# Token attention's front: weight shares split one block earlier, batch 0 values from kept transposes in two shares, two score maxima for a value tile

## What is computed

```python
def _attn_block(q_src, k_src, v_src, Wq, Wk, Wv, Wo, bo):
    q = _split_heads(q_src @ Wq)
    k = _split_heads(k_src @ Wk)
    v = _split_heads(v_src @ Wv)
    dots = jnp.einsum('bhid,bhjd->bhij', q, k) * SCALE
    attn = jax.nn.softmax(dots, axis=-1)
    out = jnp.einsum('bhij,bhjd->bhid', attn, v)
    ...
    return out @ Wo + bo
out = x1 + _attn_block(x1, x2, x2, Wq, Wk, Wv, Wo, bo)   # x2: 77 context rows
return _attn_block(out, out, x1, Wq, Wk, Wv, Wo, bo)     # 1024 tokens
```

## Time and profile before

| | |
|---|---|
| Time, median of 3 runs | 2435.78 us (2428.44 to 2436.41) |
| Time of the profiled execution | 2444.54 us |
| Its span in the trace | 2442.7 us |
| Granted TensorE clock, mean over the span | 0.964 |
| PE busy | 2296.2 us, 94% |
| DVE busy | 1509.2 us, 62% |
| ACT busy | 1107.7 us, 45% |
| POOL busy | 1062.4 us, 43% |

### The profile page before, as it was taken

How to read it: one execution, slowest core, us unless ns; L and a number is a source line. 1 busy time by engine, 2 the same in 40 slices (tenths; PEclk the granted TensorE clock), 3 DMA queues, 4 the chain that set the end, 5 groups by cost and what they waited for, 6 DMA issues and landing times.

```text
span 2442.7 us, 34142 instructions
## 1 busy us (share of the span) xinstructions
PE 2296.2 (94%) x12934; PEld 1439.0 (59%) x12934; DVE 1509.2 (62%) x2289; ACT 1107.7 (45%) x2370; POOL 1062.4 (43%) x780
## 2 busy tenths in 40 slices
PE   8999999889988999999999999999899789979998
PEld 4333443267754555555655554787566657768887
DVE  6788688267745666665666666713344566565556
ACT  2577677733323444442344444433322477643323
POOL 2556547423443888883578786333301122100000
PEclk6999999899999999999999999999899899989999
DMA  6534432232110011111011111354301511020001
GB/s 132 142 85 97 80 62 64 71 82 39 1 18 1 11 15 14 15 32 40 1 15 15 11 15 19 79 160 104 87 1 37 142 31 38 1 65 14 1 1 35
DMA packets 137805, 114.21 MB, mean 47 GB/s; under 512 B 74565, under 2 KB 114995, under 8 KB 137257
## 3 DMA queue, kind: packets, MB, share of 16 engines
q1 hardware_dynamic: 100585, 111.61, 16.8%
q0 software_dynamic: 36864, 0.15, 4.4%
q10 hardware_dynamic: 192, 0.26, 0.0%
HBM read 85.99 MB, written 13.39 MB: 41 GB/s over the span
## 4 chain that ended last, share of the span: by engine, by line
PE 76%; DMA 9%; DVE 8%; ACT 4%; issue 2%; SPq 1%; POOL 1%; ACTq 0%; POOLq 0%; DVEq 0%
PE PS L128 73%; DMA adj<-e_EE,e_IX 8%; PE PS L1287 1%; ACT a_P L884 1%; DVE c_MX L1935 1%; DVE g_SS L132 1%; PE PS L360 1%; SPq L154 1%; DVE c_AC L132 0%; DVE g_st L1378 0%; DVE a_MX L759 0%; ACT g_SS L1472 0%; PE PS L361 0%; DMA a_s<-a_OU 0%; POOL e_EQ L137 0%
## 5 line engine op out<-in xcount | busy, mean ns | idle before, releaser
L353 POOL DMA_INDIRECT adj<-e_EE,e_IX x256 | 416.1, 1625 | 416.0 <-DMA adj<-e_EE,e_IX 355.7
L1935 DVE TENSOR_REDUCE c_MX<-PS 128x2 f32<-128x1024 f32 x256 | 312.9, 1222 | 176.6 <-PE PS L128 176.4
L132 POOL TENSOR_TENSOR c_AC<-c_AC,c_P 128x1024 f32<-128x1024 f32 x145 | 364.8, 2516 | 70.7 <-DVE c_AC L132 63.9
L2032 ACT ACTIVATE c_P<-PS 128x1024 f32<-128x1024 f32 x256 | 252.0, 1026 | 215.1 <-PE PS L128 215.1
L759 DVE TENSOR_REDUCE a_MX<-PS 128x2 f32<-128x1024 f32 x256 | 304.0, 1219 | 55.6 <-PE PS L128 54.2
L884 ACT ACTIVATE a_P<-PS 128x512 f32<-128x512 f32 x512 | 270.1, 602 | 91.0 <-PE PS L128 90.0
L128 PE MATMUL PS<-c_P,c_VV 128*64 128x512 f32 x1024 | 247.7, 605 | 0.0
L137 POOL TENSOR_SCALAR e_EQ<-e_KR,e_KC 128x128 bf16<-128x128 f32 x256 | 165.0, 645 | 144.9 <-DMA e_KR<-adj_key 92.9
L128 PE MATMUL PS<-a_QS,a_KS 64*128 64x512 f32 x512 | 194.3, 464 | 11.2 <-ACT a_P L884 6.7
L128 PEld LDWEIGHTS PS<-a_QS,a_KS 64*128 64x128 f32 x512 | 84.3, 190 | 165.7 <-ACT a_P L884 97.5
L128 PE MATMUL PS<-a_KS,a_QS 48*128 48x512 f32 (+1 forms) x512 | 168.6, 473 | 11.2 <-DVE a_MX L759 11.1
(11 more groups left out here) (499 smaller groups left out, 4595.9 us busy)
## 6 DMA issues: line engine op xcount, KB each, us to landing
e_KR<-adj_key SPq DMA_DIRECT2D x64, 256.0 KB, 3.7
f_W<-in_L_ffn_w SPq DMA_DIRECT2D x16, 1024.0 KB, 7.8
c_RB<-c_r SPq DMA_DIRECT2D x58, 128.0 KB, 2.9
g_FB<-in_fside_1x16xSxS SPq DMA_DIRECT2D x8, 616.0 KB, 8.0
adj<-e_zt SPq DMA_DIRECT2D x16, 256.0 KB, 4.1
adj<-e_EE,e_IX POOLq DMA_INDIRECT x256, 3.2
d_AJ<-adj SPq DMA_DIRECT2D x8, 512.0 KB, 9.0
a_KS<-a_KH SPq DMA_DIRECT2D x30, 128.0 KB, 3.7
```

The source lines that it names most:

```text
L132: return v.e.tensor_tensor(o, a, b, op)
L353: g.e.indirect_dma_start(self.adj, bass.IndirectOffsetOnAxis(ap=self.IXE[:, k:k + 1], axis=0), self.EE[:, k:k + 1], None, compute_op=ALU.a ...
L1935: v.e.reduce_max(MX[:, w % 2, :, qt, kh], bank(0, 2).rearrange("p (h n) -> p h n", h=2), AX, negate=True).then_inc(*smax_dve.up())
L2032: s.e.activation(PB[t % NP][:, :, :].rearrange("p h n -> p (h n)"), bank(2 + 2 * (t % 2), 2), ACT.Exp, scale=0.125).then_inc(*st_act.up())
```

## The change

It makes a class `Shares` before block b, used in both blocks, and changes five things.

1. `coarse` and `fine` of the weights of P = 0 are done in block b, at i = 13 and 14 (`shares`).
2. x1's transposes of batch 0 (XT, columns 0 to 1023) are split into two shares c_XV in block b, at i = 2 to 5, 512 columns of one half of the depth at a time (`x_shares`), before c_XH takes their place. c_XV lies in a part of c_OT.
3. In the front, WV is split into shares c_WV, over the buffers c_P, in two halves of 512 columns (`split_v`), between the first preparations of keys and queries.
4. Values of batch 0 are products in shares: 6 fp32r matmuls for a tile and half. `turn_x` for batch 0 is gone. The second half is a job of its own, `prep_w`.
5. Round 0's maxima are made two for a tile, in tiles 0 to 3; `row 0` and `m 0` follow in tile 4, and round 1's first four maxima in tiles 4 to 7. The P = 1 weights are split in tiles 4 and 5.

```diff
@@ stage_ctx, schedule
+                if 2 <= i < 6:
+                    yield "x_shares", (i - 2) // 2, i % 2
+                if 13 <= i < 15:
+                    yield "shares", 14 - i
...
+class Shares:
+    def __init__(self, K):
+        W = K.over("c_WS", "LS", 0, [128, 2, 2, 2, 128])
...
+        self.XV = [K.over(f"c_XV{n}", "c_OT", 8192 * i + 8192, [128, 2, 1024]) for i, n in enumerate("HL")]
...
+    def coarse(self, s, P, w):
+        for k in range(2):
+            ins = s.e.copy(self.WS[w][0][:, k, :], self.weight(w, P, k))
+        ins.then_inc(*self.act.up())
...
+    def coarse_x(self, s, k, h):
+        cols = slice(512 * h, 512 * h + 512)
+        s.e.copy(self.XV[0][:, k, cols], self.XT[:, k, cols]).then_inc(*self.x_act.up())
+    def fine_x(self, v, k, h):
+        cols = slice(512 * h, 512 * h + 512)
+        v.wait_ge(self.x_act, 2 * k + h + 1)
+        tt(v, self.XV[1][:, k, cols], self.XT[:, k, cols], self.XV[0][:, k, cols].bitcast(F32), ALU.subtract).then_inc(*self.x_dve.up())
@@ stage_c, schedule
-        for w in (1, 0):
-            yield "coarse", 0, w
-            yield "fine", 0, w
         yield "prep_k", 0, 0
+        yield "split_v", 0
         yield "prep_q", 0
+        yield "split_v", 1
         yield "prep_k", 0, 1
         yield "prep_q", 1
         for b in range(2):
-            if b == 0:
-                yield "turn_x", b, 0
             for kt in range(8):
                 if b and kt == 0:
                     continue
-                if kt < 7:
+                if b and kt < 7:
                     yield "turn_x", b, kt + 1
                 yield "prep_v", b, kt
                 if kt < 6:
                     yield "send", 2
-                if b == 0:
-                    yield "s", 0, kt
-                    if kt >= 4:
-                        yield "s", 1, kt - 4
-            for w in (1, 0):
-                yield "coarse", 8 * b + 1, w
-                yield "fine", 8 * b + 1, w
+                if b == 0 and kt < 4:
+                    yield "s", 0, 2 * kt
+                yield "prep_w", b, kt
+                if b == 0 and kt < 4:
+                    yield "s", 0, 2 * kt + 1
+                elif b == 0:
+                    if kt == 4:
+                        yield "row", 0
+                        yield "m", 0
+                    yield "s", 1, kt - 4
+                    if kt < 6:
+                        yield "coarse", 1, 5 - kt
+                        yield "fine", 1, 5 - kt
             if b:
+                for w in (1, 0):
+                    yield "coarse", 8 * b + 1, w
+                    yield "fine", 8 * b + 1, w
                 yield "fetch", 2
-            if b == 0:
-                yield "row", 0
-                yield "m", 0
-            else:
...
@@ stage_c, tensor
+                    pe.wait_ge(K.shares.x_dve, 4)
+                    pe.wait_ge(wvl_dve, h + 1)
+                    parts = [(x[:, k, tile], W, k) for k in range(2) for x, W in (
+                        (XV[0], WVS[0]), (XV[0], WVS[1]), (XV[1], WVS[0]))]
+                    for q, (x, W, k) in enumerate(parts):
+                        ins = mm(pe, bank(bk), x, W[:, k, cols], q == 0, q == 5)
@@ stage_c, vector
+            elif kind == "split_v":
+                h, = a
+                cols = slice(512 * h, 512 * h + 512)
+                v.wait_ge(wvh_act, h + 1)
+                tt(v, WVS[1][:, :, cols], W0.WV[:, :, cols], WVS[0][:, :, cols].bitcast(F32), ALU.subtract).then_inc(*wvl_dve.up())
@@ stage_c, scalar
+            elif kind == "split_v":
+                h, = a
+                cols = slice(512 * h, 512 * h + 512)
+                s.e.copy(WVS[0][:, :, cols], W0.WV[:, :, cols]).then_inc(*wvh_act.up())
```

More of the change, by code:

```diff
@@ L1378, in vector @@
                     v.e.reduce_max(m, ss[:, :, :], AX, negate=True).then_inc(*max_dve.up())
+            elif kind == "shares":
+                K.shares.fine(v, 0, a[0])
+            elif kind == "x_shares":
+                K.shares.fine_x(v, *a)
             elif kind == "soft":
@@ L1462, in scalar @@
                 s.e.copy(*united(b, q, 1, bk)).then_inc(*u_act.up())
+            elif kind == "shares":
+                K.shares.coarse(s, 0, a[0])
+            elif kind == "x_shares":
+                K.shares.coarse_x(s, *a)
             elif kind == "exp":
@@ L1583, in stage_c @@
     MT = sb(c, "c_MT", [8, 2, 128], F32R)
-    split_w = K.over("c_WS", "LS", 0, [128, 2, 2, 2, 128])
-    WS = [[split_w[:, w, part, :, :] for part in range(2)] for w in range(2)]
+    WS, ws_dve = K.shares.WS, K.shares.dve
+    XV, WVS = K.shares.XV, [K.over(f"c_WV{n}", "c_P0", 8192 * i, [128, 2, 1024]) for i, n in enumerate("HL")]
     XH = [K.coarse[:, k, :] for k in range(2)]
@@ L1872, in tensor @@
                 free[bk] = (xv_act, nth[job])
-            elif kind == "prep_v":
+            elif kind in ("prep_v", "prep_w"):
                 b, kt = a
                 xk = halves(K.LS[:, kt % 4, :])
[L1876 to L1882, removed]
+                h = int(kind == "prep_w")
+                bk = 2 + 2 * (kt % 2) + h
+                cols = slice(512 * h, 512 * h + 512)
+                bank_free(bk)
+                if b:
+                    pe.wait_ge(xv_act, kt + 1)
+                    mm(pe, bank(bk), xk[:, 0, :], W0.WV[:, 0, cols], True, False)
+                    ins = mm(pe, bank(bk), xk[:, 1, :], W0.WV[:, 1, cols], False, True)
+                else:
+                    tile = slice(128 * kt, 128 * kt + 128)
+                    pe.wait_ge(K.shares.x_dve, 4)
[4 more added lines that the diff above has]
+                        ins = mm(pe, bank(bk), x, W[:, k, cols], q == 0, q == 5)
+                ins.then_inc(*v_pe.up())
+                free[bk] = (v_dve if h else v_act, nth[job])
             elif kind == "out":
@@ L1917, in vector @@
                 P, w = a
[L1918 to L1921, removed]
+                K.shares.fine(v, P, w)
+            elif kind == "split_v":
[3 more added lines that the diff above has]
+                tt(v, WVS[1][:, :, cols], W0.WV[:, :, cols], WVS[0][:, :, cols].bitcast(F32), ALU.subtract).then_inc(*wvl_dve.up())
             elif kind == "prep_k":
@@ L2006, in scalar @@
                     s.wait_ge(q_pe, 2 * P)
[L2007 to L2011, removed]
+                if P == 9:
+                    s.wait_ge(v_pe, 32)
+                K.shares.coarse(s, P, w)
+            elif kind == "split_v":
+                h, = a
+                cols = slice(512 * h, 512 * h + 512)
+                s.e.copy(WVS[0][:, :, cols], W0.WV[:, :, cols]).then_inc(*wvh_act.up())
             elif kind == "prep_k":
@@ L3572, in build @@
             K.consts = Consts(K)
+            K.shares = Shares(K)
             stage_ctx(K, block, "b_", 0.125, K.W0)
```

24 lines of the change are left out of this document (17 added, 7 removed).

## The result

| | before | after |
|---|---|---|
| Time, median | 2434.7 us (4 runs, 2428.44 to 2436.41) | 2409.09 us (4 runs, 2406.71 to 2414.06) |
| Ratio | | 0.9898, 95% interval 0.9872 to 0.9925 |
| Profiled execution, its span | 2444.54, 2442.7 us | 2408.95, 2407.2 us |

A forecast was written before the change was run, and what follows sets the result against it. PE was taken as the bound, with 76% of the last-ending chain; a gain of 16.2 us before round 0 and 4.7 in it, say 21, takes 2435.78 to 2415 us, range 2408 to 2424.

The forecast's parts named there:

- The start: Token front's beginning: without the first weights' split there, PE starts at about 701.9 instead of 703.00, gaining 1.1 us.
- The values' start: Before the first value tile: waits of 1.40 and 0.24 us and the transposes go; delay from WV's split taken as 0.
- Tiles 0 to 3: Front's first four value tiles: 2.04 us a half, 4.08 a tile, 16.3 us in all, no wait for maxima counted.
- Rival 1: Maxima bind: each half in tiles 0 to 3 waits some 0.5 us for its bank; 5 us go, 2420; chance 0.10.
- Tiles 4 to 7: Front's last four value tiles: 3.48 us each, 13.9 us, plus a 1.1 us wait for the row of maxima.
- Round 0: To the turn of round 1's maxima: no c_MR wait, clock up; 12.8 us instead of 17.55, saving 4.7.
- Rival 2: The clock drops once more and round 0 keeps its slow stretch: about 3 us, 2418; chance 0.08.
- Block b: Added casts and subtractions lie where PE is full and ACT and DVE have room: counted as 0 us.
- Rival 3: Block b stretches as DVE's additions enter its loop, costing 4 to 7 us: 2419 to 2422; chance 0.06.
- POOL: The 14 gathers ahead of its first addition: cover shrinks from 25 to 4 us, and nothing waits.
- rival 4: Gathers fall behind additions and hold POOL: 4 to 8 us given back, 2419 to 2423; chance 0.06.
- Rival 6: The dense group never brings up the clock: 28 us more than forecast, 2443; chance 0.02.

The follow-up runs named there:

- e1: Changed kernel with the P = 0 weights split at the start of the token stage again: start 3.60 us instead of 2.37, stretch 54.89 us against 53.42.
- e5: Changed kernel with the row of maxima and its turn moved behind the eighth tile, at the front's end: stretch 59.37 us against 53.42.
- e7: Changed kernel with five unused fp32 products in PE's wait for the barrier after block b: stretch 52.18 us against 53.42.
- e8: Changed kernel with the row and turn between tile 4's value halves, plus five unused products in the barrier wait: 2411.66 us, ratio 0.9900 to the kernel before.

## Why the prediction was right, step by step

- **The start**, 1.1 us: measured 1.22 (e1: 1.23).
- **The values' start**, 2.3 us of waits and turns: they went whole. "Keys" fell by 2.78. The 24 products took 7.63 instead of 8.46 us, as the slow clock lasted less, by chance; and 0.35 us went to a wait that I had put at nothing. The split of WV was in time for the values, and took the median price, not the worst, but the queries' fine part stood behind it on DVE, and PE waited for that at 696.67:

```profile
694.79 1.23 DVE L132 TENSOR_TENSOR c_WVL<-b_WV,c_WVH 128x1024 fp32r<-128x1024 f32 x1 [0.18 <-ACT c_WVH L2073]
695.93 0.68 DVE L132 TENSOR_TENSOR c_QL<-PS,c_QH 128x512 fp32r<-128x512 f32 x1
696.53 1.22 DVE L132 TENSOR_TENSOR c_WVL<-b_WV,c_WVH 128x1024 fp32r<-128x1024 f32 x1
```

```profile
696.06 1.55 POOL L353 DMA_INDIRECT adj<-e_EE,e_IX  x1 [2.07 <-DMA adj<-e_EE,e_IX]
```

  I had asked only whether the split delays the values and the first maximum, not whether it delays the bank of the next product. The rule on shared SBUF interfaces (Trainium skill, GPSIMD Engine Reference, 1. Specifications) did not bite here: the second subtraction ran beside a gather's issue and took 1.22 us all the same. Beside POOL's own multiplication, in round 15, it did, up to 3.59 us.
- **Tiles 0 to 3**, 16.3 us: measured 16.04 (698.18 to 714.22). Rival 1, maxima that bind, did not come, but by a hair. DVE's rows, and the pair that the second reduction lets go:

```profile
701.77 0.69 DVE L2035 COPY c_VV<-PS 128x512 f32<-128x512 f32 x1 [0.36 <-PE PS L128]
702.38 1.22 DVE L1995 TENSOR_REDUCE c_MX<-PS 128x2 f32<-128x1024 f32 x1
```

```profile
703.67 0.50 PE L128 MATMUL PS<-c_KH,c_QH 64*128 64x512 f32 x2
```

  The reduction ends at 703.60 and the pair starts at 703.67, just as PE is through with the half ahead of it.
- **Tiles 4 to 7**, 13.9 + 1.1: measured 14.5 in all. The term was 0.5 too high: a tile's twelve products take 2.91 us (722.08 to 724.99), where I had 3.05.
- **Round 0**, 12.8: measured 12.54, and 5.0 saved instead of 4.7. Rival 2, a further fall of the clock, did not come; in e5, with the turn at the front's end and a wait of 1.56 us, it does.
- **Block b**, 0: 164.3 us before, 164.2 after. Rival 3 is out, also at three times the work.
- **POOL**: its first addition waits 1.23 us, not 25:

```profile
742.25 4.84 POOL L132 TENSOR_TENSOR c_AC<-c_AC,c_P 128x1024 f32<-128x1024 f32 x2 [1.23 <-DVE c_AC L132]
```

  I had counted on 4 us of margin. Of the 2.8 that are missing, 1.6 are the addition itself, which comes 22.6 us earlier and not 21, and 1.2 the gathers: from the first issue to the last they take 47.0 us (692.44 to 739.47) instead of 45.9. It was still enough, so rival 4 stayed away.
- **Rival 6**, a clock that never rises: 1.00 in 695 to 714. The Trainium skill (TensorE: Matmul & The Clock Gate, A second HAM failure mode: psum-queue depth-cycling) describes a swing that did not occur on this single bank pair in the changed kernel.

The terms add up to 22.6 against 20.9 forecast; 0.8 of the 1.7 between them is the slow clock, and so luck. The median fell by 25.6; the other 3 us are inside the interval, and no place in the traces shows them as the change's: from the turn of round 1's maxima to the last c_XF product both take 320.4 us, and what differs elsewhere (stage a, the stage of gathers: 313 to 322 us from the last c_OT to the next block's d_EN in all runs) differs among executions of like code.

## What to carry to other kernels

A maximum, a row or a transfer that a round needs should be spread over the work ahead at the rate at which its one consumer can take it (here one reduction of 1.22 us for each 2.04 us of PE), not bunched at the end: that, with the row sent as soon as its maxima are there, gave 12.2 of 22.6 us. Price a stall with what it does to the clock behind it; in e5 2.5 us more went behind a wait of 1.6. When work is added to an engine ahead of a need, look at what stands behind it in that engine's order too: the split of WV was in time for its own reader and late for the next product. When the run-to-run scatter is larger than the edit, compare a stretch between two landmarks in the trace.

## What was not expected of the hardware

- Five products without use, 2.3 us in a barrier's wait, kept TensorE at 2.4 GHz and made the next 24 products 0.5 to 1.8 us faster (e7, e8: 6.71 us both times).
- A DVE addition with two SBUF inputs, 1.22 us in the median, was never stretched by POOL's gather issue (341 times, at most 1.29 us), but 185 times by POOL's own additions and multiplications: each time it ended 1.08 to 1.09 us after POOL's operation. The longest took 3.59 us and held PE for 1.30 us.
